# Keys made once per batch in the second cross attention, and the turned means copied by ScalarE

## The chip, the cores and the metric

The kernel runs on one core of a Trainium2 chip. The core has TensorE (matrix products), VectorE, ScalarE (activations) and GpSimd, and SyncE, which here only issues DMAs. Matmuls write PSUM, which has eight banks of 512 float32 per partition; everything else lives in SBUF, 128 partitions. The metric is the device time of one execution in microseconds.

## The reference, cut to what matters

Two layers, each an attention, a cross attention over a context, and a feed-forward part, with layer norms between. The input is 8 batches of 56 tokens of width 128; the context `ctx_512` is 8 batches of 1500 rows of width 64. The change is in the cross attention of the second layer and in what prepares it. With 16 heads of 8 key columns each:

```
qh = (q @ Wq + bq).reshape(B, LQ, HEADS, D_K).transpose(0, 2, 1, 3)
kh = (k @ Wk + bk).reshape(B, LKV, HEADS, D_K).transpose(0, 2, 1, 3)
vh = (v @ Wv + bv).reshape(B, LKV, HEADS, D_K).transpose(0, 2, 1, 3)
scores = jnp.einsum('bhqd,bhkd->bhqk', qh, kh) * (1.0 / np.sqrt(D_K))
attn = jax.nn.softmax(scores, axis=-1)
out = jnp.einsum('bhqk,bhkd->bhqd', attn, vh)
return concat @ Wo + bo
```

## The kernel before, in words

Everything runs in one program, stage after stage; each engine has its own written order, and semaphores tie them. The two cross attentions are two objects of the class `Cross` (L916): `cross1` (first layer) and `cross2` (second layer, `biased`). Both run over 8 batches of 12 chunks; a chunk is 125 context rows against all 16 x 56 = 896 queries.

Keys are never made. The key weights are folded into the queries: the query unit ("Q", L1003) multiplies each head's queries by its key weights, giving 64 rows (and one for the bias), and scores are products of these with the turned context (64 x 1500 per batch). For precision both sides are split in a high and a low bf16 part, stacked on the rows: one matmul of 128 rows and one of 65 (97 in `cross2`), each in two halves of 448 columns (L1125), four per chunk.

In chunk n, TensorE (`run_pe`, L1094) waits for the exp of chunk n-2, issues the scores of n, and then the value sums (`pv`, L1054) of chunk n-2: fourteen matmuls on the high part of the probabilities (L1066, L1068) and seven on the low part (L1073). ScalarE takes the exp (L1206). The low part of the probabilities is made on GpSimd or VectorE (`low_part`, L1226); `low_on_pool` says by whom (in `cross2` before: VectorE in chunks 0, 1 and 11 of a batch). Four buffers (`RING`) hold probabilities.

Between, side units for the next batch are placed by hand (`placement`, L896), each in one of three side banks taken in turn, where a unit waits until the unit three places ahead has been read: queries ("Q"), 21 maxima ("M", a matmul of 500 columns, L1024, and a VectorE reduction, L1241), the shift by the maximum ("A", L1030 and L1253), and for the batch before the turned means ("N", L1036; VectorE copies them, L1270) and the output projection ("O", L1042; copy L1274). The mean itself (`mean`, L1278: L1282 and L1286) is VectorE's, and TensorE starts the value sums of a batch only when it is done.

`cross2` needs the turned context in bf16 parts: SyncE loads it (`turned_in`, L1982), ScalarE copies it (`context_act`, L1182 and L1183), and VectorE or GpSimd makes its low part (`context_low`, L1191). For batches 0 and 1 that is done in the last batch of `cross1`, in chunks 2 to 9. The front of a cross attention (`front_pe`, `front_dve_run`) makes queries and maxima of batch 0 before its first chunk; `keep_warm` (L212) are matmuls whose results nobody reads.

## Time and profile before

| | us |
|---|---|
| median of 3 runs | 669.24 (666.65 to 669.37) |
| the profiled execution's own time | 664.66 |
| its span, first to last instruction | 662.9 |
| first cross attention, last batch | about 300 to 323 |
| second cross attention, front | about 409 to 428 |
| second cross attention, 8 batches | about 428 to 627 |

Times in a row are microseconds from the start of the span. A row of the timeline gives start, duration, engine, line, operation, tiles, and the number of instructions merged in it. The duration of a matmul has a modelled end; distances between starts are the safer reading.

### The profile page before, as it was taken

The numbers are of one execution on the slowest core, as the hardware profiler recorded it, in microseconds if no ns is written. First come the engines' busy times: TensorE is split into PE (matmuls) and PEld (weight loads), VectorE is DVE, ScalarE is ACT, GpSimd is POOL, SyncE is SP. The second block draws the span as 40 slices with busy tenths as digits, with TensorE's granted clock in tenths as the row PEclk, the third lists the DMA queues.
The fourth block names the chain that finished last, engine by engine and source line by source line (L and its number), as shares of the span: only waits on it lengthen the run. The fifth ranks groups of instructions, "written<-read, shape, count | busy, mean of one in ns | idle before, by whom it ended". The sixth has DMA issues, their size and how long they took to land.

```text
span 662.9 us, 19804 instructions
## 1 busy us (share of the span) xinstructions
PE 621.5 (94%) x8743; PEld 464.5 (70%) x8743; DVE 493.9 (75%) x796; ACT 353.0 (53%) x550; POOL 379.3 (57%) x272
## 2 busy tenths in 40 slices
PE   8889898899999999999898979999999999999997
PEld 4566785677777777777776556677777777777774
DVE  3666738799989889896665764877888988977543
ACT  2065663655646646647354316286586586664443
POOL 1362453388888888574220326078988988955400
PEclk9999999999999999999999999999999999999999
DMA  9600003000000002000032000001101100000000
GB/s 267 244 1 3 3 2 134 2 2 3 2 2 2 2 2 95 4 2 2 1 132 120 1 0 1 1 2 48 48 2 49 48 2 2 2 2 2 2 1 15
DMA packets 4657, 20.87 MB, mean 31 GB/s; under 512 B 500, under 2 KB 756, under 8 KB 4572
## 3 DMA queue, kind: packets, MB, share of 16 engines
q1 hardware_dynamic: 4572, 19.60, 8.8%
q8 instruction: 69, 1.13, 0.7%
q14 instruction: 16, 0.13, 0.1%
HBM read 19.37 MB, written 0.23 MB: 30 GB/s over the span
## 4 chain that ended last, share of the span: by engine, by line
PE 72%; DVE 12%; ACT 8%; issue 5%; POOL 2%; DMA 1%; POOLq 0%; DVEq 0%
PE psum L1125 18%; PE psum L1024 10%; PE psum L1066 5%; PE psum L1073 5%; PE psum L212 5%; PE psum L1068 5%; DVE scratch L1241 3%; PE psum L1003 3%; PE psum L1030 1%; PE psum L241 1%; PE psum L1042 1%; POOL scratch L626 1%; ACT scratch L1159 1%; ACT lv L286 1%; PE psum L1036 1%
## 5 line engine op out<-in xcount | busy, mean ns | idle before, releaser
L1226 POOL TENSOR_TENSOR scratch<-scratch 125x896 bf16<-125x896 f32 x136 | 238.5, 1765 | 117.7 <-ACT scratch L1206 117.5
L1206 ACT ACTIVATE scratch<-psum 125x896 f32<-125x896 f32 x192 | 173.1, 915 | 147.0 <-PE psum L1125 145.8
L1241 DVE TENSOR_REDUCE scratch<-psum 128x1 f32<-128x500 f32 x336 | 209.8, 671 | 14.1 <-PE psum L1024 6.4
L1125 PE MATMUL psum<-scratch 128*125 128x448 bf16 (+2 forms) x624 | 143.6, 355 | 0.5 <-ACT scratch L1206 0.2
L1066 PE MATMUL psum<-tok,scratch 125*128 125x65 bf16 x1344 | 108.9, 195 | 1.8 <-DVE kT L1286 1.8
L1068 PE MATMUL psum<-tok,scratch 125*128 125x64 bf16 x1344 | 108.3, 192 | 0.0
L1066 PEld LDWEIGHTS psum<-tok,scratch 125*128 125x128 bf16 x1344 | 95.3, 97 | 15.6 <-issue 2.6
L1024 PE MATMUL psum<-scratch 128*128 128x500 bf16 x273 | 102.3, 375 | 3.3 <-DVE scratch L1241 2.0
L1068 PEld LDWEIGHTS psum<-tok,scratch 125*128 125x128 bf16 x1344 | 90.2, 99 | 16.1
L1125 PEld LDWEIGHTS psum<-scratch 128*125 128x125 bf16 (+2 forms) x624 | 80.0, 136 | 26.1 <-ACT scratch L1206 0.8
L1226 DVE TENSOR_TENSOR scratch<-scratch 125x896 bf16<-125x896 f32 x56 | 68.6, 1227 | 18.1 <-ACT scratch L1206 17.0
L212 PE MATMUL psum<-w_second 128*128 128x256 bf16 x597 | 79.0, 272 | 0.0
L1073 PE MATMUL psum<-tok,scratch 125*128 125x65 bf16 x1344 | 72.5, 194 | 2.8 <-POOL scratch L1226 1.6
L1073 PEld LDWEIGHTS psum<-tok,scratch 125*128 125x128 bf16 x1344 | 61.1, 98 | 16.8 <-POOL scratch L1226 2.4
L212 PEld LDWEIGHTS psum<-w_second 128*128 128x128 bf16 x597 | 56.7, 97 | 19.4 <-issue 7.4
L1024 PEld LDWEIGHTS psum<-scratch 128*128 128x128 bf16 x273 | 26.3, 96 | 11.5 <-DVE scratch L1241 3.8
L1125 PE MATMUL psum<-scratch,nrm 128*125 128x448 bf16 (+1 forms) x144 | 33.2, 356 | 0.0
L1236 DVE TENSOR_TENSOR scratch<-psum,scratch 64x448 bf16<-64x448 f32 x28 | 17.2, 617 | 16.1 <-ACT scratch L1159 16.0
L1353 POOL CAST tok<-raw 125x384 bf16<-125x384 f32 x16 | 13.4, 836 | 27.3 <-DVE xo L1834 12.5
L281 ACT ACTIVATE sq<-psum 128x224 f32<-128x224 f32 (+2 forms) x24 | 8.6, 357 | 36.6 <-PE psum L241 36.4
L1024 PE MATMUL psum<-nrm,scratch 128*128 128x500 bf16 x63 | 23.6, 375 | 1.2 <-DVE scratch L1236 0.6
L1125 PEld LDWEIGHTS psum<-scratch,nrm 128*125 128x125 bf16 (+1 forms) x144 | 18.1, 136 | 5.3
(337 smaller groups left out, 896.7 us busy)
## 6 DMA issues: line engine op xcount, KB each, us to landing
nrm<-turned_dram SPq DMA_DIRECT2D x8, 750.0 KB, 4.6
raw<-ctx_dram SPq DMA_DIRECT2D x4, 672.0 KB
w_third<-fifth_dram SPq DMA_DIRECT2D x3, 636.0 KB, 5.4
w_third<-third_dram SPq DMA_DIRECT2D x2, 844.0 KB, 21.1
w_third<-third_dram SPq DMA_DIRECT2D x2, 843.5 KB, 19.2
w_fourth<-fourth_dram SPq DMA_DIRECT2D x3, 542.5 KB, 5.7
w_first<-first_dram SPq DMA_DIRECT2D x1, 996.0 KB, 4.8
w_second<-second_dram SPq DMA_DIRECT2D x1, 834.0 KB, 6.7
```

The lines of the kernel that those rows point to most:

```text
L212: nc.tensor.matmul(bank(b, 256), constant[:, 0:128], constant, start=True, stop=True)
L1003: mm = nc.tensor.matmul(psum[0:65, self.home(idx + half), 56 * n:56 * n + 56], par(self.wk, 65 * h, 65 * h + 65)[rows, :], qT[rows, j, 56 ...
L1024: mm = nc.tensor.matmul(bank(B, TB), CR["qa", i][:, 128 * r:128 * r + 128], CR["ya", self.context_of(b)][:, TB * t:TB * t + TB], start=Tru ...
L1066: nc.tensor.matmul(psum[:, sums, 65 * r:65 * r + 65], rows, t[:, c, 64:129], start=(c == 0 and r == 0), stop=False, skip_group_check=True)
L1068: nc.tensor.matmul(psum[:, sums, 65 * r:65 * r + 64], rows, t[:, c, 0:64], start=False, stop=False, skip_group_check=True)
L1073: mm = nc.tensor.matmul(psum[:, sums, 65 * r:65 * r + 65], CR["pl"][0:CP, n % RING, 128 * r:128 * r + 128], t[:, c, 64:129], start=False, ...
L1125: mm = nc.tensor.matmul(bank(S + f, HALF, CP), lhs[0:rows, CP * c:CP * c + CP], rhs[0:rows, HALF * f:HALF * f + HALF], start=(rows == 128) ...
L1206: nc.scalar.activation(CR["p"][0:CP, n % RING, :].rearrange("p (f n) -> p f n", f=2), psum[0:CP, S:S + 2, 0:HALF], ACT.Exp).then_inc(self. ...
L1226: ops.tensor_tensor(CR["pl"][0:CP, n % RING, :], CR["p"][0:CP, n % RING, :], p_high(n % RING), ALU.subtract).then_inc(done, 1)
L1236: nc.vector.tensor_tensor(CR["qb", i][0:64, cols], bank(B, HALF, 64), CR["qa", i][0:64, cols], ALU.subtract).then_inc(self.aux_freed, 1)
L1241: nc.vector.tensor_reduce(mxp[:, r, t:t + 1], bank(B, TB), X_AXIS, ALU.max).then_inc(self.aux_freed, 1)
L1353: nc.gpsimd.tensor_copy(tok[i][:, lot, 64:128], src).then_inc(self.tok_high, 1)
```

## The change

In the second cross attention the keys are made: per batch, three matmuls of 500 columns ("K": `x_wk` by the turned context, float32) give 128 rows, 16 heads of 8. ScalarE adds the bias and writes the high bf16 part, VectorE the low part. SyncE then copies them from SBUF to SBUF into four groups of four heads; a group has 96 rows (32 high, 32 low, 32 high again) and a row of ones for the shift. That is twelve copies per third of a batch, 36 per batch. The queries are no longer folded with the key weights: a matmul with a constant ("spread") puts them in the same 96 rows, masked so that a head meets only its own 8 rows. Scores are four matmuls of 97 rows and 224 columns per chunk. Maxima have tiles of 112 queries, eight in place of seven, so 24 units per batch. The keys of batch b+2 are made in batch b (two in chunk 0, one in chunk 9); those of batches 0 and 1 in chunks 6 to 11 of the last batch of the first cross attention, where `context_act` and `context_low` go. TensorE waits there for all six residues before the value sums of the last two chunks. The turned means are copied by ScalarE. GpSimd has the low part of chunk 1 too, and its memsets for the rows of ones go. The fifth pack of weights shrinks. `cross1` keeps its own way of working.

The diff's core:

```diff
-        def low_on_pool(n):
+        def low_on_pool(n, keyed):
+            if keyed:
+                return n % 2 == 0 if n >= CHUNKS * (BATCH - 1) + 3 else n % CHUNKS not in (0, 11)
             return n % 2 == 0 if n >= CHUNKS * (BATCH - 1) + 3 else n % CHUNKS not in (0, 1, 11)
-        def placement(front, outputs, turns):
+        def keyed_placement(front, outputs, keys):
+            at = [[] for _ in range(CHUNKS)]
+            maxima = iter(KEYED[2:2 + MAXIMA * TBLK])
+            def some(c, n):
+                at[c] += [[u] for u in itertools.islice(maxima, n)]
+            if keys:
+                at[0] += [[("K", 0)], [("K", 1)]]
+            if front:
+                at[1] += [KEYED[0:2]]
+                some(2, 3)
+                some(3, 1)
+            if outputs:
+                at[3] += [[]] * (not front) + [[("N", 0)], [("N", 1)]]
+            if front:
+                some(3, 1)
+                for c in range(4, 11):
+                    some(c, 3 if c < 9 else 2)
+                at[11] += [[], [KEYED[-2]], [KEYED[-1]]]
+            if outputs:
+                at[5] += [[("O", 0)]]
+            if keys:
+                at[9] += [[("K", 2)]]
+            return at
...
                 if kind == "Q":
                     if b:
                         self.wait_freed(pe, idx - 2)
-                    else:
+                    elif not self.keyed:
                         pe.wait_ge(self.yb_set, 2)
+                    if self.keyed:
+                        for g in range(GROUPS):
+                            mm = nc.tensor.matmul(psum[0:96, self.home(idx + g // 2), 224 * (g % 2):224 * (g % 2) + 224],
+                                                  par("spread", 96 * g, 96 * g + 96), qT[:, :, 56 * b:56 * b + 56],
+                                                  start=True, stop=True)
+                            if g % 2:
+                                mm.then_inc(self.aux_ready, 1)
+                        return
...
+                elif kind == "K":
+                    mm = self.keys_pe(pe, b, k, B)
+                elif kind == "M" and self.keyed:
+                    t, r = k // MAXIMA, k % MAXIMA
+                    if k == 0 and b:
+                        pe.wait_ge(self.q_high, 2 * b)
+                    elif k == 0:
+                        pe.wait_ge(self.front_act, 1)
+                        pe.wait_ge(self.front_dve, 1)
+                    if r == 0:
+                        pe.wait_ge(keys_loaded[i][t], 192 * (b // 2 + 1))
+                    mm = nc.tensor.matmul(bank(B, TB, QROWS), CR["qa", i][0:64, QROWS * r:QROWS * r + QROWS],
...
+                                          key_group(i, r // 2)[0:64, TB * t:TB * t + TB], start=True, stop=True)
...
+            def keys_pe(self, pe, b, t, B):
+                if b == 0:
+                    pe.wait_ge(loaded["keys"], 16)
+                pe.wait_ge(turned_loaded[t], 16 * (b + 1))
+                return nc.tensor.matmul(bank(B, TB), par("x_wk", rows=64), turned[:, TB * t:TB * t + TB],
+                                        start=True, stop=True)
+            def keys_act(self, act, b, t, B):
+                cols = slice(TB * t, TB * t + TB)
+                if b:
+                    act.wait_ge(keys_loaded[(b - 1) % 2][t], 192 * ((b - 1) // 2 + 1))
+                nc.scalar.activation(key_high[:, cols], bank(B, TB), ACT.Identity, bias=col("x_bk")
+                                     ).then_inc(keys_high, 1)
+            def keys_dve(self, dve, b, t, B):
+                cols = slice(TB * t, TB * t + TB)
+                dve.wait_ge(keys_high, TBLK * b + t + 1)
+                nc.vector.scalar_tensor_tensor(key_low[:, cols], bank(B, TB), col("x_bk"), key_high[:, cols], ALU.add,
+                                               ALU.subtract).then_inc(keys_low, 1)
...
+                        for g in range(GROUPS):
+                            mm = nc.tensor.matmul(psum[0:CP, S + g // 2, 224 * (g % 2):224 * (g % 2) + 224],
+                                                  key_group(i, g)[0:97, CP * c:CP * c + CP],
+                                                  CR["qa", i][0:97, 224 * g:224 * g + 224], start=True, stop=True)
...
+                    if self is cross1 and b == BATCH - 1 and c >= 6:
+                        kb, t = (c - 6) // TBLK, (c - 6) % TBLK
+                        if kb:
+                            pe.wait_ge(keys_low, t + 1)
+                        else:
+                            self.wait_freed(pe, self.index("O", 0, BATCH - 2))
+                        cross2.keys_pe(pe, kb, t, SIDE[t]).then_inc(keys_made, 1)
+                if self is cross1:
+                    pe.wait_ge(keys_low, 2 * TBLK)
...
-                        nc.scalar.activation(CR["qb", i][96:97, cols], psum[64:65, B, 0:HALF], ACT.Copy)
-                    nc.scalar.activation(CR["qa", i][0:64, cols], bank(B, HALF, 64), ACT.Copy)
-                    ins = nc.scalar.activation(CR["qa", i][64:128, cols], bank(B, HALF, 64), ACT.Copy)
+                    ins = nc.scalar.activation(CR["qa", i][0:64, cols], bank(B, HALF, 64), ACT.Copy)
+                    if not self.keyed:
+                        ins = nc.scalar.activation(CR["qa", i][64:128, cols], bank(B, HALF, 64), ACT.Copy)
                     ins.then_inc(self.q_high, 1)
+                elif kind == "K":
+                    act.wait_ge(self.aux_ready, idx + 1)
+                    self.keys_act(act, b, k, B)
+                elif kind == "N" and self.keyed:
+                    act.wait_ge(self.aux_ready, idx + 1)
+                    if k == 0 and b:
+                        act.wait_ge(self.aux_ready, self.index("O", 0, b - 1) + 1)
+                    lo, hi = (0, 512) if k == 0 else (512, 896)
+                    nc.scalar.activation(usb[0:64, lo:hi], bank(B, hi - lo, 64), ACT.Copy).then_inc(self.mean_turned, 1)
...
-                    if self is cross1 and b == BATCH - 1 and c in (2, 4, 6, 8):
-                        cross2.context_act(act, (c - 2) // 4, (c - 2) // 2 % 2)
-                    if self is cross2 and b < BATCH - 2 and c in (4, 6):
-                        self.context_act(act, b + 2, c // 2 - 2)
+                    if self is cross1 and b == BATCH - 1 and c >= 6:
+                        act.wait_ge(keys_made, c - 5)
+                        cross2.keys_act(act, (c - 6) // TBLK, (c - 6) % TBLK, SIDE[(c - 6) % TBLK])
...
-                elif kind == "N":
+                elif kind == "N" and not self.keyed:
...
+                    if self is cross1 and b == BATCH - 1 and c >= 6:
+                        cross2.keys_dve(dve, (c - 6) // TBLK, (c - 6) % TBLK, SIDE[(c - 6) % TBLK])
...
-                    if self is cross2 and b < BATCH - 2 and c in (5, 8):
-                        self.context_low(pool, nc.gpsimd, b + 2, c // 3 - 1)
...
-            def turned_in(b):
-                sp.dma_start(turned[b % TURNED], packs["turned"][:, CTX * b:CTX * b + CTX]
-                             ).then_inc(turned_loaded[b % TURNED], 16)
+            def turned_in(b, t):
+                cols = slice(TB * t, TB * t + TB)
+                sp.dma_start(turned[:, cols], packs["turned"][:, CTX * b + TB * t:CTX * b + TB * t + TB]
+                             ).then_inc(turned_loaded[t], 16)
+            def keys_in(b, t):
+                cols = slice(TB * t, TB * t + TB)
+                for g in range(GROUPS):
+                    rows = slice(32 * g, 32 * g + 32)
+                    for k, part in enumerate((key_high, key_low, key_high)):
+                        sp.dma_start(key_group(b % 2, g)[32 * k:32 * k + 32, cols], part[rows, cols]
+                                     ).then_inc(keys_loaded[b % 2][t], 16)
+            sp.wait_ge(cx_var, 4)
+            sp.dma_start(params["keys"], packs["keys"]).then_inc(loaded["keys"], 16)
+            for t in range(TBLK):
+                turned_in(0, t)
             sp.wait_ge(cross1.tok_set, 2 * BATCH)
-            for b in range(TURNED):
-                turned_in(b)
+            for i in range(2):
+                sp.dma_start(flat[96:97, 2 * CTX * i:2 * CTX * i + 2 * CTX], packs["ones_row"]).then_inc(ones_loaded, 16)
+            for b in range(2):
+                for t in range(TBLK):
+                    sp.wait_ge(keys_low, TBLK * b + t + 1)
+                    turned_in(b + 1, t)
+                    keys_in(b, t)
...
+            for b in range(2, BATCH):
+                for t in range(TBLK):
+                    if t != 1:
+                        for lot in (0, 1) if t == 0 else (2,):
+                            sp.wait_ge(keys_low, TBLK * b + lot + 1)
+                            if b < BATCH - 1:
+                                turned_in(b + 1, lot)
+                    sp.wait_ge(cross2.scores, CHUNKS * (b - 2) + 4 * t + 4)
+                    keys_in(b, t)
```

## Rows read from the trace of the kernel before

**Rows 1.** The page: busy time by engine, and the chain that ended last

```profile
PE 621.5 (94%) x8743; PEld 464.5 (70%) x8743; DVE 493.9 (75%) x796; ACT 353.0 (53%) x550; POOL 379.3 (57%) x272
...
PE 72%; DVE 12%; ACT 8%; issue 5%; POOL 2%; DMA 1%; POOLq 0%; DVEq 0%
```

**Rows 2.** Busy time in two batches: stretch, length, engines, clock, DMA share, GB/s

```profile
482.51:507.96 25.45, 25.11 (x407) 18.79 (x404) 21.70 (x35) 17.08 (x23) 22.92 (x15) 1.00 0.11 33
507.96:533.40 25.44, 25.10 (x407) 18.79 (x405) 21.73 (x35) 17.08 (x23) 22.93 (x15) 1.00 0.11 32
```

**Rows 3.** Timeline of TensorE, chunks with three maxima

```profile
491.64 0.38 PE L1024 MATMUL psum<-scratch 128*128 128x500 bf16 x1
492.28 0.38 PE L1024 MATMUL psum<-scratch 128*128 128x500 bf16 x1
492.50 0.37 PE L1073 MATMUL psum<-tok,scratch 125*128 125x65 bf16 x7
492.71 0.38 PE L1024 MATMUL psum<-scratch 128*128 128x500 bf16 x1
492.92 0.92 PE L1125 MATMUL psum<-scratch 128*125 128x448 bf16 x4
493.68 0.37 PE L1024 MATMUL psum<-scratch 128*128 128x500 bf16 x1
```

**Rows 4.** Timeline of VectorE in one batch, and its low parts by line

```profile
486.73 1.14 DVE L1270 COPY scratch<-psum 64x512 f32<-64x512 f32 x2
487.79 3.58 DVE L1241 TENSOR_REDUCE scratch<-psum 128x1 f32<-128x500 f32 x6
...
492.05 10.09 DVE L1241 TENSOR_REDUCE scratch<-psum 128x1 f32<-128x500 f32 x15 [0.37 <-PE psum L1024]
...
L1226 DVE TENSOR_TENSOR scratch<-scratch 125x896 bf16<-125x896 f32 x56 | 68.6, 1227 | 18.1 <-ACT scratch L1206 17.0
```

**Rows 5.** Timeline of TensorE: float32 matmuls, two instructions each

```profile
334.13 3.29 PE L735 MATMUL psum<-xn,w_third 128*128 128x224 f32 x16 [0.45 <-DVE xn L695]
337.26 3.19 PE L740 MATMUL psum<-kT,w_third 128*128 128x224 f32 x16
...
507.13 1.16 PE L1003 MATMUL psum<-qT,w_third 64*65 64x56 f32 x32
```

**Rows 6.** Timeline of VectorE and ScalarE: nearest operations, and the front

```profile
407.29 0.57 DVE L2150 SCALAR_TENSOR_TENSOR t<-psum,w_fourth,t 128x336 f32<-128x336 f32 x1 [0.16 <-PE psum L758]
411.63 0.62 DVE L1297 TENSOR_TENSOR scratch<-psum,scratch 64x448 bf16<-64x448 f32 x1
...
420.39 1.85 DVE L1241 TENSOR_REDUCE scratch<-psum 128x1 f32<-128x500 f32 x3 [0.38 <-PE psum L1024]
...
508.87 0.54 ACT L1158 ACTIVATE scratch<-psum 64x448 bf16<-64x448 f32 x1
```

**Rows 7.** Timeline of GpSimd: low parts and a context part

```profile
492.11 1.61 POOL L1191 TENSOR_TENSOR nrm<-nrm 64x750 bf16<-64x750 f32 x1
493.69 4.96 POOL L1226 TENSOR_TENSOR scratch<-scratch 125x896 bf16<-125x896 f32 x3
508.24 2.35 POOL L1226 TENSOR_TENSOR scratch<-scratch 125x896 bf16<-125x896 f32 x1 [0.32 <-ACT scratch L1206]
```

**Rows 8.** Timeline of TensorE, last batch of the first cross attention

```profile
310.47 0.95 PE L1125 MATMUL psum<-scratch 128*125 128x448 bf16 x4
311.89 0.95 PE L1125 MATMUL psum<-scratch 128*125 128x448 bf16 x4
322.71 0.39 PE L1073 MATMUL psum<-tok,scratch 125*128 125x65 bf16 x7 [0.97 <-DVE scratch L1226]
```

**Rows 9.** SyncE: issues in the timeline, durations by line, time to landing

```profile
L1983 SPq DMA_DIRECT2D nrm<-turned_dram x8: 327/328/502, 253.8 to 525.7; - x8
...
340.97 1.91 SPq L1970 DMA_DIRECT2D w_third<-fifth_dram  x4
...
out_dram<-t SPq DMA_DIRECT2D x2, 112.0 KB, 1.7
```

321 lines of the change are left out of this document (167 added, 154 removed).

## The prediction

> **What bounds the kernel now.** I read first the busy shares and the chain that ended last: TensorE is busy 94% of the span and carries 72% of the chain [rows 1]. Then the stretches by stage. Each of the middle batches of the second cross attention takes 25.45 us, to the hundredth, and in one of them TensorE is busy 25.11 us, GpSimd 22.92, VectorE 21.70 and ScalarE 17.08 [rows 2]. So that stage is TensorE's, with VectorE and GpSimd close behind. Modelled ends make a matmul's own duration useless here (0.19 us for 65 columns); I use distances between starts. A run of starts in the maxima [rows 3] gives: one maxima matmul of 500 columns 0.21 us, the seven low value matmuls 0.22, the four score matmuls of 448 columns 0.76. The fourteen high value matmuls take 0.43: two maxima matmuls with them between start 0.64 apart [rows 3]. A chunk with three maxima is then 0.76 + 0.43 + 0.22 + 0.63 = 2.04 us, and VectorE's 15 reductions in 10.09 us (0.67 each) follow that pace; its own pace, where matmuls lie ready, is six in 3.58 us, 0.60 each [rows 4]. Keep that number: three reductions are 1.79 us.
>
> **The change in the steady batches.** Matmuls first, TensorE's sum for one batch with keys.
> - Scores: four matmuls of 224 columns in place of four of 448. At 0.19 per 448 columns [rows 3] a half is 0.095, a chunk 0.385 in place of 0.76. Twelve chunks: -4.5 us.
> - Maxima: 24 in place of 21, three times 0.21: +0.6.
> - Queries: the old unit's 32 instructions take 1.16 us, some 1.1 without the modelled end [rows 5]. The new one is four float32 matmuls of 224 columns; sixteen instructions of 224 columns, two per matmul, span 3.13 us (334.13 to 337.26), 0.39 per matmul [rows 5], so 1.56: +0.5.
> - Keys ("K", three per batch, owners 2 to 7): float32, 500 columns, 0.39 x 500 / 224 = 0.87 each: +2.6.
> Sum -0.8 us of 25.45. The maxima for the shift, the turned means and the output stay as they are.
>
> VectorE: 24 reductions in place of 21, +1.8; three key residues. The trace has no such instruction; the nearest are 0.57 us for the same operation on 336 columns and 0.62 for a subtraction from PSUM on 448 [rows 6]; I take 0.70 each (0.6 to 0.8), +2.1. One low part fewer (1.23 in the mean [rows 4]), -1.2, and no turned means (1.14 for both [rows 4]), -1.1. So 21.7 becomes 23.3. ScalarE has two copies of queries in place of six, at 0.54 for 448 columns [rows 6], loses the context copies, and gains three key copies and the two means, about 0.6 each by the same row: 17.1 [rows 2] less 2.2 plus 3.0 less the context copies, so under 18; it costs nothing, but it now stands between TensorE and the next use of a side bank. It copies the means after the exp of chunk 3; the exp behind it, of chunk 4, is not needed for two more chunks, so I cost the move from VectorE at nothing. Without that cover it would cost 1.1 us a batch. GpSimd gains one low part (1.66) and loses two context parts of 1.6 [rows 7]: even.
>
> Now the waits. In the maxima chunks TensorE needs 0.385 + 0.65 + 0.63 = 1.67, VectorE 1.79, GpSimd 1.66 [rows 4, 7]: VectorE falls about 0.12 behind per chunk and is some 1.1 us late when the shift is asked for, of which about 0.5 us shows. At the start of a batch two keys (1.74) and the queries come before any value sum; the mean waits on VectorE behind a low part and two residues, and the old cover (the queries stood between the last value sum and the first of the next batch) is gone: another 0.5 or 0.6. Against about 1.15 us of such holes today (25.45 less 24.3 of matmul demand by the prices above), I get 25.25 per batch, -0.2 (bounds -1.5, if the holes don't grow, to +0.8, if VectorE's lag is paid in full). The six batches 0 to 5 have keys: -1.3 in all. Batch 6 has none: 2.6 us less, -2.8. Batch 7 has neither keys nor maxima: today 1.42 us per chunk by the prices above, now 1.04, twelve chunks, less what the mean and GpSimd's low parts (1.66 each [rows 7]) hold up: -3.7. The front has three more reductions, 1.8 us, less 0.3 for shorter query work, and the four late query matmuls shrink to one, which takes away most of the waits for TensorE that VectorE has there (0.38 us and two shorter ones [rows 6], 0.9 in all): +0.6. **Second cross attention: -7.2 us.**
>
> **The change in the last batch of the first cross attention.** Here keys of batches 0 and 1 are made from chunk 6 on, six units, and the sums of chunks 10 and 11 now wait for the sixth residue. Follow it by the clock. The scores of chunk 6 start at 310.47 and those of chunk 7 at 311.89 [rows 8]. The first key matmul would run 311.9 to 312.8, its copy (0.6) end at 313.5, its residue at 314.3. Only then does SyncE start. Per third of a context it issues one load and twelve copies of 32 rows, and it takes the next third only when all thirteen are out. The copy of key (1, t) waits until the twelve of (0, t) have landed, because they read the same buffer. So 39 issues stand between the first residue and the last copy. What does an issue cost? No transfer of this size from SBUF to SBUF is in the trace. But of all SyncE's issues none is under 0.327 us, whether 78 KB or 996 KB, 8 loads of contexts have a median of 0.328, and back to back four take 1.91, 0.47 each [rows 9]. I take 0.42 (0.37, the least with the step between, to 0.47). 39 x 0.42 = 16.4: the last is out at 330.7 and lands 1.7 us after its issue, as the outputs do [rows 9], at 332.0. Then ScalarE's copy 0.6, VectorE's residue 0.7 and 0.1 of signals: 333.4. The sums of two chunks, 1.3: 334.7. Today the last of them starts at 322.71 and takes 0.22 [rows 8]. **+11.8 us.** It is all on the path: the mean, the projection and the next stage hang on it. Bounds of the issue alone: +9.8 to +13.7. What was there, four pairs of context copies on ScalarE and four subtractions on VectorE, goes; that is inside the sum, which starts from 310.47.
> In the second attention the same 39 issues (16.4 us) fit in a batch of 25 and are asked for a batch later: no cost. If an issue took over 0.64 us they would bind there as well.
>
> The Trainium skill, "DMA: Bandwidth & Descriptors", section "Issuing engines are not separate DMA queues", says that the sequencer's time to initiate a DMA is "usually small relative to the DMA itself". By that rule the 39 issues would fall away beside the landings, and the result would be rival 1's; the SyncE rows above speak against it, at 0.33 us and more.
>
> **Sum.** -7.2 + 11.8 = +4.6. The profiled execution took 664.66 us (span 662.9): 669.3. The median of the three runs is 4.6 above it, at 669.24: **673.8 us**. A difference of 0.5%, 3.3 us, is about what a measurement of this kernel can tell.
>
> **The rivals.**
> 1. *Issues of small copies are cheap* (0.1 us or so). Then the tail is set by TensorE: six chunks of 1.42 + 0.87 = 2.29 from 310.47 end at 324.2, then copy, residue and sums: 326.9, +4.0 and not +11.8. Sum -3.2: 666.0, faster than before. It decides below 0.2 us per issue (39 x 0.2 = 7.8 is about the matmuls' own pace). For: each copy has 32 rows of 1,000 bytes, a quarter of the others' rows. Against: no row under 0.327 whatever the size. 0.22.
> 2. *The batches gain more*: holes don't grow, 24.3 per batch, -0.95 more for each of six. Sum -1.1: 668.1. For: TensorE's demand falls by 0.8, and VectorE has queues of three banks. Against: VectorE's 23.3 plus its waits for ScalarE. 0.12.
> 3. *The batches don't gain*: VectorE, now with 24 reductions, becomes the bound in full, or the low parts on GpSimd, which take 2.35 us and not 1.66 beside VectorE's own [rows 7], hold chunk 1 to 3. +1 per batch for six: 679.8. A variant of the same sign: TensorE stands idle for some 5 us before 333.4 and comes back at its half clock, 1.2 GHz; all rows of before show a granted clock of 1.00 in the cross attentions, so no row prices it; doubling the 1.3 of sums and part of the projection behind it is +1.5 to +3. 0.16.
> 4. Main case, 0.50. Within it the issue's 0.37 to 0.47 and a few tenths per batch give +1 to +8.
>
> **How the numbers follow.** Main case: slower 0.36, same 0.14. Rival 1: faster 0.12, same 0.10. Rival 2: faster 0.06, same 0.06. Rival 3: slower 0.16. Together faster 0.18, same 0.30, slower 0.52. Range: down to 664.5 for rival 1 with batches a little better, up to 680 for rival 3. The main case's own: 670 to 677.
>
> **What would show it.** SyncE: some 290 more issues; their mean, and the distance between twelve of them, decides. In the first attention's last batch: TensorE idle of 4 to 6 us ahead of the last sums, released by the key residue, and ScalarE's key copies waiting for transfers. Batch distance in the second: 25.2, then 22.6, then some 17.8. VectorE's reductions at 0.60 throughout. The turned means on ScalarE with no added wait for them on TensorE. I am wrong if the last sums of the first attention start before 328, or if a batch falls under 24.5 or rises above 26.

## The result, and the profile after

| | before | after |
|---|---|---|
| median | 668.83 us (666.65 to 669.37) | 728.48 us (727.36 to 729.32) |
| ratio, 95% interval | | 1.090 (1.087 to 1.093) |
| span of the profiled execution | 662.9 | 726.6 |

The change makes the kernel 9% slower. The forecast was 673.8, slower by 0.7%; the sign was right and the size wrong by a factor of more than ten. The two medians differ by 59.7 us and the two spans by 63.7; the profiled execution of before was one of its quick ones (664.66 us).

The page of after, busy time by engine and chain by engine and line; it answers to [rows 1]:

```profile
PE 673.5 (93%) x8630; PEld 476.0 (66%) x8630; DVE 510.7 (70%) x815; ACT 335.9 (46%) x528; POOL 360.8 (50%) x263
...
PE 76%; DVE 10%; ACT 5%; issue 3%; SPq 3%; POOL 1%; DMA 1%; DVEq 0%; POOLq 0%; ACTq 0%
PE psum L1069 9%; PE psum L1216 8%; PE psum L1150 6%; PE psum L1157 6%; PE psum L1207 6%; PE psum L216 6%; PE psum L1152 5%; PE psum L1080 4%; SPq L2101 3%; PE psum L1116 3%; DVE scratch L1327 2%; PE psum L1036 2%; PE psum L1099 2%; PE psum L1105 1%; POOL scratch L630 1%
```

TensorE has 113 matmuls fewer in the profile than before (some records can be missing) and is busy 52 us longer. Two lines are new at the head of the chain: the maxima of the second cross attention (L1069, 9%) and SyncE's copies of the keys (SPq L2101, 3%).

Where the time went is read from one instruction per batch, VectorE's reciprocal at the start of the mean, and from two other reciprocals of VectorE that bound the stretch behind the first cross attention (335.93 in before, 361.76 in after) and the start of the second one's front (391.36 and 417.19). The differences between their starts give the account; "first" and "second" are the cross attentions.

| stretch | before | after | difference |
|---|---|---|---|
| up to the last batch of the first | 303.13 | 304.98 | +1.9 |
| last batch of the first | 20.01 | 42.10 | +22.1 |
| the stretch behind it | 12.79 | 14.68 | +1.9 |
| front and batch 0 of the second | 64.83 | 77.17 | +12.3 |
| the next five batches | 127.27 | 153.27 | +26.0 |
| batch 6 | 25.45 | 27.28 | +1.8 |
| batch 7 | 18.16 | 15.89 | -2.3 |

The stretch between the two bounds is 55.43 us in both, and the batches of the first cross attention ahead of its last are alike to 0.1 us. The 1.9 us of the first line are there already at the first of these reciprocals, which starts at 151.62 in after, at 149.75 in before, and between 149.47 and 151.06 in the other kernels below, some of them with the whole change in them. So they look like the scatter of single executions. The busy time of the engines in a steady batch of after (columns as in [rows 2], which it answers):

```profile
525.42:556.47 31.05, 30.66 (x387) 19.96 (x386) 24.18 (x37) 14.70 (x20) 20.30 (x15) 1.00 0.20 52
```

TensorE is busy for 30.66 of 31.05 us, at full clock. So the batches did not grow by waits: the matmuls themselves take longer than the prices that were read from before. The one wait of TensorE above 0.2 us in such a batch is for the mean, in its timeline:

```profile
526.43 0.19 PE L1150 MATMUL psum<-tok,scratch 125*128 125x65 bf16 x1 [0.29 <-DVE kT L1367]
```

The timeline of TensorE in after, in a chunk with three maxima (it answers to [rows 3]):

```profile
540.96 0.60 PE L1207 MATMUL psum<-scratch,nrm 97*125 97x224 bf16 x4
541.49 0.41 PE L1069 MATMUL psum<-nrm,scratch 64*112 64x500 bf16 x1
541.84 0.20 PE L1150 MATMUL psum<-tok,scratch 125*128 125x65 bf16 x1
...
542.25 0.19 PE L1152 MATMUL psum<-tok,scratch 125*128 125x64 bf16 x1
542.37 0.41 PE L1069 MATMUL psum<-nrm,scratch 64*112 64x500 bf16 x1
542.72 0.39 PE L1157 MATMUL psum<-tok,scratch 125*128 125x65 bf16 x7
543.03 0.41 PE L1069 MATMUL psum<-nrm,scratch 64*112 64x500 bf16 x1
543.38 0.41 PE L1207 MATMUL psum<-scratch,nrm 97*125 97x224 bf16 x2
```

From the start of a maxima matmul to the start of the next instruction are 0.35 us, where before had 0.21; and the seven low value matmuls take 0.31 before the next maxima matmul may start, in place of 0.21 to 0.22. The chunk takes 2.42 us (540.96 to 543.38). The forecast had 1.67 for TensorE and 1.79 for VectorE. What is new in the shape is the first number: a maxima matmul now has 64 rows, and its neighbours 97 or 125.

The other loss is in the last batch of the first cross attention. SyncE's issues there, in the timeline of after (start, duration, then how many are merged):

```profile
316.44 0.48 SPq L2092 DMA_DIRECT2D w_first<-turned_dram  x1
316.96 8.25 SPq L2101 DMA_DIRECT2D nrm<-scratch  x12
325.26 0.59 SPq L2092 DMA_DIRECT2D w_first<-turned_dram  x1
325.89 7.56 SPq L2101 DMA_DIRECT2D nrm<-scratch  x12
333.49 0.59 SPq L2092 DMA_DIRECT2D w_first<-turned_dram  x1
334.13 7.56 SPq L2101 DMA_DIRECT2D nrm<-scratch  x12
```

All issues of that line (least, median and most, in ns), the answer to [rows 9]:

```profile
L2101 SPq DMA_DIRECT2D nrm<-scratch x288: 507/591/1847, 317.0 to 650.3; - x144
```

Three of ScalarE's key copies wait for these transfers, 4.63, 6.77 and 6.74 us (the last one here, in the timeline of after), and the first value sum of the last two chunks, in TensorE's, waits for the last residue:

```profile
343.06 0.68 ACT L1123 ACTIVATE scratch<-psum,w_first 128x500 bf16<-128x500 f32 x1 [6.74 <-DMA nrm<-scratch]
```

```profile
344.57 0.24 PE L1150 MATMUL psum<-tok,scratch 125*128 125x65 bf16 x1 [6.13 <-DVE scratch L1129]
```

The busy time and the clock in four stretches of 10 us of after (the third number from the right is the granted clock):

```profile
310.00:320.00 10.00, 10.00 (x151) 6.37 (x147) 5.07 (x6) 5.73 (x7) 3.91 (x3) 1.00 0.08 21
320.00:330.00 10.00, 6.10 (x55) 3.29 (x54) 2.56 (x3) 3.08 (x4) 2.81 (x2) 0.84 0.23 61
330.00:340.00 10.00, 4.96 (x28) 2.59 (x27) 1.83 (x2) 1.49 (x2) 0.00 (x0) 0.50 0.23 60
340.00:350.00 10.00, 5.43 (x51) 5.15 (x52) 1.57 (x3) 0.68 (x1) 0.00 (x0) 0.50 0.22 56
```

TensorE stands idle for 8.9 of the 20 us from 320 to 340, and its granted clock goes to 0.50, the 1.2 GHz level, and is still there when the sums and the projection run after 344.57.

### The profile page after: what moved, and what is told of

It reads as the page before. It is cut to its first block, busy times and chain, and to the rows that moved or that the text cites. A ratio compares the mean times of both kernels' runs of the same rounds, so it can differ in the third digit from the quotient of the medians.

```text
span 726.6 us, 19924 instructions
## 1 busy us (share of the span) xinstructions
PE 673.5 (93%) x8630; PEld 476.0 (66%) x8630; DVE 510.7 (70%) x815; ACT 335.9 (46%) x528; POOL 360.8 (50%) x263
## 4 chain that ended last, share of the span: by engine, by line
PE 76%; DVE 10%; ACT 5%; issue 3%; SPq 3%; POOL 1%; DMA 1%; DVEq 0%; POOLq 0%; ACTq 0%
PE psum L1069 9%; PE psum L1216 8%; PE psum L1150 6%; PE psum L1157 6%; PE psum L1207 6%; PE psum L216 6%; PE psum L1152 5%; PE psum L1080 4%; SPq L2101 3%; PE psum L1116 3%; DVE scratch L1327 2%; PE psum L1036 2%; PE psum L1099 2%; PE psum L1105 1%; POOL scratch L630 1%
## 5 line engine op out<-in xcount | busy, mean ns | idle before, releaser
L1327 DVE TENSOR_REDUCE scratch<-psum 112x1 f32<-112x500 f32 (+1 forms) x360 | 232.2, 674 | 35.2 <-PE psum L1069 26.2
L1216 PE MATMUL psum<-scratch 65*125 65x448 bf16 (+1 forms) x384 | 89.3, 358 | 0.1
L1069 PE MATMUL psum<-nrm,scratch 64*112 64x500 bf16 x192 | 79.7, 415 | 0.3 <-issue 0.3
L1157 PEld LDWEIGHTS psum<-tok,scratch 125*128 125x128 bf16 x1344 | 57.6, 98 | 25.4 <-issue 16.4
L1310 DVE TENSOR_TENSOR scratch<-scratch 125x896 bf16<-125x896 f32 x48 | 59.8, 1247 | 12.9 <-ACT scratch L1291 12.3
L1080 PE MATMUL psum<-scratch 128*128 128x500 bf16 x168 | 62.9, 375 | 2.1 <-DVE scratch L1327 2.0
L1216 PEld LDWEIGHTS psum<-scratch 65*125 65x125 bf16 (+1 forms) x384 | 49.3, 137 | 19.8 <-ACT scratch L1291 3.0
L1207 PE MATMUL psum<-scratch,nrm 97*125 97x224 bf16 x384 | 55.0, 268 | 0.3 <-DVE scratch L1335 0.3
L1207 PEld LDWEIGHTS psum<-scratch,nrm 97*125 97x125 bf16 x384 | 37.0, 136 | 15.9 <-issue 14.5
L1129 DVE SCALAR_TENSOR_TENSOR scratch<-psum,w_first,scratch 128x500 bf16<-128x500 f32 x24 | 17.7, 738 | 35.9 <-ACT scratch L1123 35.6
L1069 PEld LDWEIGHTS psum<-nrm,scratch 64*112 64x112 bf16 x192 | 23.6, 123 | 21.2 <-issue 6.5
L1116 PE MATMUL psum<-w_first 64*128 64x500 f32 x48 | 28.0, 668 | 7.4 <-DVE scratch L1129 3.9
```

The lines of the kernel that those rows point to most:

```text
L1069: mm = nc.tensor.matmul(bank(B, TB, QROWS), CR["qa", i][0:64, QROWS * r:QROWS * r + QROWS], key_group(i, r // 2)[0:64, TB * t:TB * t + TB] ...
L1080: mm = nc.tensor.matmul(bank(B, TB), CR["qa", i][:, 128 * r:128 * r + 128], CR["ya", i][:, TB * t:TB * t + TB], start=True, stop=True)
L1116: return nc.tensor.matmul(bank(B, TB), par("x_wk", rows=64), turned[:, TB * t:TB * t + TB], start=True, stop=True)
L1157: mm = nc.tensor.matmul(psum[:, sums, 65 * r:65 * r + 65], CR["pl"][0:CP, n % RING, 128 * r:128 * r + 128], t[:, c, 64:129], start=False, ...
L1207: mm = nc.tensor.matmul(psum[0:CP, S + g // 2, 224 * (g % 2):224 * (g % 2) + 224], key_group(i, g)[0:97, CP * c:CP * c + CP], CR["qa", i][ ...
L1216: mm = nc.tensor.matmul(bank(S + f, HALF, CP), lhs[0:rows, CP * c:CP * c + CP], rhs[0:rows, HALF * f:HALF * f + HALF], start=(rows == 128) ...
```

## The experiments

The theory made from the two traces: the loss is (a) about 0.23 us for each maxima matmul, because its 64 rows stand between matmuls of over 64, and (b) an issue of a copy from SBUF to SBUF takes 0.63 us on SyncE and not 0.42, in a chain of 39 that halts TensorE. Rivals: maxima or scores are slowed by where they read or write (the keys now lie in the token buffer, filled by transfers), by VectorE, or by the copies' traffic; and the turned means on ScalarE hold the side banks. Each kernel is compared with executions of the kernel before on the same chip (medians 667.2 to 667.7).

One thing has to be known for all of them. Many of these kernels show short stretches at the 1.2 GHz level, most of them 3 to 4 us long, and they don't come in the same places: before with its maxima over 64 rows has one at 332 to 336, and the kernel behind it, with the same code there, has none at that place but one at 396 to 400. Most of them cost 1 to 1.6 us. So distances are compared where the granted clock is 1.00, and where it isn't the text says so.

### Maxima over 96 rows

After, with the maxima over 96 rows of the same keys and queries; the rows 64 to 95 add the low part of the products, so the maxima must wait for the queries' low parts.

```diff
-  CR["qa", i][0:64, QROWS * r:QROWS * r + QROWS], key_group(i, r // 2)[0:64, TB * t:TB * t + TB]
+  CR["qa", i][0:96, QROWS * r:QROWS * r + QROWS], key_group(i, r // 2)[0:96, TB * t:TB * t + TB]
```

> The changed kernel, with the maxima matmuls over 96 rows of queries and keys in place of 64 (the low rows of the queries join; TensorE waits for them ahead of the first maximum). Theory A, a matmul over 64 rows between matmuls over more rows costs TensorE about 0.23 us more than its columns do: each of the 24 maxima per batch goes from 0.44 to 0.21 us, 5.5 us less per batch, so the distance of two batches falls from 31.05 to about 25.5, and the whole to about 690 us. Rival B, the 36 copies per batch from SBUF to SBUF, or their reading, slow TensorE or the reductions: the copies are the same here, so the distance stays at 31 and the whole at 728. The halt ahead of the last sums of the first attention (to 347) stays under both.

Measured: 703.6 us, ratio 1.054 (1.047 to 1.060); span 701.0, 25.6 less than after. TensorE's timeline in this kernel, one chunk with three maxima:

```profile
523.94 0.55 PE L1207 MATMUL psum<-scratch,nrm 97*125 97x224 bf16 x4
524.32 0.38 PE L1069 MATMUL psum<-nrm,scratch 96*112 96x500 bf16 x1
524.97 0.40 PE L1069 MATMUL psum<-nrm,scratch 96*112 96x500 bf16 x1
525.42 0.40 PE L1069 MATMUL psum<-nrm,scratch 96*112 96x500 bf16 x1
525.65 0.55 PE L1207 MATMUL psum<-scratch,nrm 97*125 97x224 bf16 x4
```

1.71 us in place of 2.42, and the prediction's 1.67 for TensorE is confirmed: the same matmul of 500 columns with half as many rows again is cheaper by 0.71 / 3 = 0.24 us. Batches take 27.71, 3.35 less. They don't take 25.3: TensorE is busy 25.22, and the maxima now wait for the queries' low parts, once a batch, in this kernel's timeline (0.55 more is a wait for the shift; with 64 rows after has neither):

```profile
542.27 0.39 PE L1069 MATMUL psum<-nrm,scratch 96*112 96x500 bf16 x1 [1.94 <-DVE scratch L1377]
```

### Maxima over 64 rows in the kernel before

The same thing from the other side: nothing of the change, only the maxima of the second cross attention over the rows 64 to 127 (the low part of the context is left out of them).

```diff
-  CR["qa", i][:, 128 * r:128 * r + 128], CR["ya", self.context_of(b)][:, TB * t:TB * t + TB]
+  rows = slice(64, 128) if self.biased else slice(0, 128)
...
+  CR["qa", i][rows, 128 * r:128 * r + 128], CR["ya", self.context_of(b)][rows, TB * t:TB * t + TB]
```

> The kernel before, with one size changed: the maxima of the second cross attention are taken over 64 rows (the high parts alone, so the shift is a little off the true maximum) in place of 128. No key copies exist here. Theory A: 21 x 0.23 = 4.8 us more per batch, distance 25.45 to about 30.3 for the seven batches with maxima, the whole from 669 to about 703. Rival B: half the rows cost nothing, distance 25.45 or below, 669.

Measured: 699.7 us in one execution, span 697.9, 35 us over before. Batches take 29.70 in place of 25.45: 4.25 / 21 = 0.20 us per maxima matmul. The front and batch 0 take 72.78 in place of 64.83, so the front loses 3.7 as well. Its stretch behind the first attention is 1.05 longer too (13.84, granted 0.88), which is one of the low stretches and not the maxima. No key, no copy between buffers and no other place of operands is in this kernel, so (a) needs none of them.

### The matmuls around them over 64 rows too

Is it the change between shapes, or is a 64-row matmul slow? In the front of the kernel before, three unread matmuls of `keep_warm` stand between two maxima. Here they have 64 rows like the maxima.

```diff
-  nc.tensor.matmul(bank(b, 256), constant[:, 0:128], constant, start=True, stop=True)
+  nc.tensor.matmul(bank(b, 256), constant[rows, 0:128], constant[rows], start=True, stop=True)
...
-  keep_warm(3 if k else 8, 2 if self.biased else 6)
+  keep_warm(3 if k else 8, 2 if self.biased else 6, rows=slice(64, 128) if self.biased else slice(0, 128))
```

> The kernel before with the second cross attention's maxima over 64 rows (as e2_before_max64), and the three unread matmuls that stand between two maxima in the front over 64 rows too. Starts of the front's maxima are 0.54 us apart with 128 rows everywhere and 0.75 where only the maxima have 64 rows. Theory 'a change of the number of row groups costs, about 0.1 us each way': with both at 64 rows the distance returns to 0.54 (at most 0.60), while the batches behind, where the maxima still stand between wider matmuls, stay at 29.7 us. Rival 'a maxima matmul over 64 rows is slow in itself, or its operands in this place are': the distance stays at 0.75 or grows to 0.8 and more, since the others are narrow now as well. The whole is some 3.5 us under e2_before_max64's 699.7: 696 by the first, 700 or more by the second.

TensorE's timeline in the front, of the kernel with 64 rows in the maxima alone, and of the one with 64 rows in all:

```profile
414.24 0.38 PE L1025 MATMUL psum<-scratch 64*128 64x500 bf16 x1
414.56 0.50 PE L212 MATMUL psum<-w_second 128*128 128x256 bf16 x3
414.99 0.38 PE L1025 MATMUL psum<-scratch 64*128 64x500 bf16 x1
```

```profile
414.20 0.37 PE L1025 MATMUL psum<-scratch 64*128 64x500 bf16 x1
414.41 0.48 PE L212 MATMUL psum<-w_second 64*128 64x256 bf16 x3
414.74 0.37 PE L1025 MATMUL psum<-scratch 64*128 64x500 bf16 x1
```

0.75 us from one maximum to the next becomes 0.54, exactly the distance in before with 128 rows everywhere. The maxima matmul is the same in both, 64 rows from the same place; only its neighbours differ. So the price is for the change between 64 rows and more (96 to 128 in these kernels), some 0.1 us each way, and not for the 64 rows. The batches stay at 29.7, as expected.

The whole took 699.4 (one execution, span 697.6), 0.3 under the other kernel and not 3.5, and front and batch 0 together fell only from 72.78 to 71.58. The maxima don't miss the gain. From the first of the front's 21 maxima matmuls to the last are 14.23 us here (413.66 to 427.89), 17.59 in the other kernel (413.49 to 431.08) and 13.05 in before (411.81 to 424.86): 3.36 us were won, as expected. The 1.2 over before fit the four late query matmuls of 128 rows between them, where the rows still change: two maxima with one of those between stand 1.40 apart here and 1.10 to 1.12 in before. What was won was lost outside the maxima, in two stretches at the 1.2 GHz level that this execution has and the other doesn't. Their clock in this kernel (the third number from the right):

```profile
396.00:398.00 2.00, 2.00 (x11) 1.22 (x10) 1.47 (x4) 0.61 (x2) 0.28 (x1) 0.56 0.00 0
432.00:434.00 2.00, 2.00 (x8) 1.17 (x6) 0.00 (x0) 0.80 (x1) 0.00 (x0) 0.55 0.00 0
```

The first lies ahead of the maxima, in code that is the same in both, and counted from the start of the front they begin 0.95 us later; the second lies between the last maximum and the first value sum, which are 8.27 us apart in place of 7.06. That is 2.2 of the 3.4 us. So the time of one execution would have spoken against the theory, and the distances between starts decide for it.

The Trainium skill, "TensorEngine Tiling (Array Packing)", section "Key Properties", has a line that fits: "Changing tiling mode (not just tile) drains the TensorE". The traces show a cost of 0.1 us and a little more at each change between 64 rows and more, as such a drain would give. That a plain matmul over 64 rows is such a change of mode no run here shows. The prediction did not use this line.

### Key matmuls over 128 rows

After, with the key matmul over 128 rows, of which the 64 added ones meet weights of zero.

```diff
-  par("x_wk", rows=64), turned[:, TB * t:TB * t + TB]
+  par("x_wk"), params["first"][:, TB * t:TB * t + TB]
```

> The changed kernel, the 24 key matmuls over 128 rows (64 of them meet weights of zero) in place of 64. Theory A: each of them is followed and preceded by matmuls over more rows; by 0.2 us each, 0.6 per batch with keys, distance 31.05 to 30.45, and 5 us less in the whole at most, about 723. If the surcharge for the narrow form is bound to short bf16 matmuls only, nothing: 728.

Measured: 724.5 us in one execution, span 722.7. Batches take 30.63, 0.42 less for three keys: 0.14 each. From start to start a key matmul takes 0.92 us (512.33 to 513.25) in place of 1.03 (545.47 to 546.50). The same cost as with the maxima: 0.09 to 0.11 behind each key and 0.08 to 0.09 ahead of two of them; the first key of a batch, behind a matmul of the shift, starts 0.29 behind it in both kernels and shows none ahead.

### A buffer of its own for the second batch of keys

After, but the keys of batch 1 have parts of their own, so that their copies on ScalarE wait for no transfer, and all three context loads go ahead of the 36 copies of batch 0.

```diff
-                if b:
-                    act.wait_ge(keys_loaded[(b - 1) % 2][t], 192 * ((b - 1) // 2 + 1))
+                if b == 2:
+                    act.wait_ge(keys_loaded[0][t], 192)
+                elif b > 2:
+                    act.wait_ge(keys_loaded[(b - 1) % 2][t], 192 * ((b - 1) // 2 + 1))
```

> The changed kernel, but the keys of batch 1 get a buffer of their own and SyncE issues the three context loads of batch 1 ahead of the copies of batch 0, so nothing in the last batch of the first attention waits for SyncE's 39 issues. Theory C, the issues (0.63 us each) are the whole of the halt: the mean after the last sums starts at about 329 in place of 347, the half clock between 327 and 350 goes, 18 to 20 us less, about 709. Rival D, the key units themselves or ScalarE's order hold that batch: less than 5 us gained. The batch distance in the second attention stays 31 under both.

Measured: 712.4 us, ratio 1.067 (1.060 to 1.073), span 711.3. The last batch of the first attention takes 26.87 in place of 42.10, the stretch behind it 13.40 in place of 14.68; busy time and clock in the first of them in this kernel, and below it SyncE's issues in its timeline:

```profile
303.70:330.57 26.87, 24.41 (x341) 16.99 (x341) 13.56 (x17) 13.23 (x16) 9.00 (x5) 0.96 0.12 33
```

```profile
320.83 24.46 SPq L2108 DMA_DIRECT2D nrm<-scratch  x36
```

The 36 issues still take 24.46 us, but nobody waits for them. So 15.2 of the 22.1 us were the wait for the copies and what it did to the clock, 16.5 with the stretch behind. The 6.9 that are left are longer matmuls, since TensorE is busy 24.41 in place of 17.21: six keys (6 x 1.03 = 6.2), and about one more by a stretch at the 1.2 GHz level that remains (granted 0.55 from 328 to 330). The next kernels, with keys over 128 rows and a clock of 1.00 there, have 24.5.

### What an issue costs

The kernel before with more transfers on SyncE at a time when it has nothing to do (their data are not used): twelve loads from HBM and twelve copies from SBUF to SBUF, all of 32 rows of 1,000 bytes, three copies of 128 rows, and four of 32 rows of 3,000 bytes.

```diff
+            for k in range(3):
+                for rows in four:
+                    sp.dma_start(block[k][rows], packs["turned"][rows, 250 * k:250 * k + 250]).then_inc(probed, 16)
...
+                    sp.dma_start(block[3 + k][rows], block[k][rows]).then_inc(probed, 16)
...
+                sp.dma_start(block[k], block[3 + k]).then_inc(probed, 16)
...
+                sp.dma_start(flat[rows, 3 * CTX + 750:3 * CTX + 1500], flat[rows, 3 * CTX:3 * CTX + 750]).then_inc(probed, 16)
```

> The kernel before, with extra DMAs on SyncE at about 255 us where it has 86 us to wait: 12 loads from HBM of 32 rows x 1,000 bytes, then 12 copies from SBUF to SBUF of the same form, 3 copies of 128 rows x 1,000 bytes, 4 copies of 32 rows x 3,000 bytes, each group after the one before has landed. What sets SyncE's issue time? If the form from SBUF to SBUF does: 0.33 to 0.47 for the loads, 0.63 for all copies. If the number of rows or bytes does: copies of 128 rows differ from those of 32. If only the length of the queue does: the first issues of each group near 0.35, the later ones longer, whatever the form. The time of the whole stays at 669.

Issues of the four kinds in this kernel (least, median and most, in ns):

```profile
L1994 SPq DMA_DIRECT2D nrm<-turned_dram x12: 421/424/1449, 255.2 to 261.7; - x12
L1998 SPq DMA_DIRECT2D nrm<-nrm x12: 559/591/1729, 263.6 to 271.7; - x12
L2001 SPq DMA_DIRECT2D nrm<-nrm x3: 518/601/603, 273.5 to 274.7; - x3
L2004 SPq DMA_DIRECT2D nrm<-nrm x4: 556/592/593, 278.5 to 280.3; - x4
```

A load costs 0.42, a copy between places in SBUF 0.59, whether it has 32 rows or 128, 1,000 bytes a row or 3,000. For copies the size doesn't matter; the longest issue in each of the two groups of twelve takes 1.4 and 1.7 us. The price of the prediction, 0.42, is right for this load, which is the form that its rows had. The form is not all, though: SyncE's loads of a third of the context take 0.59 (median) between copies in after, and 0.47, the same instruction, in the kernel by way of HBM that has no such copies; the whole contexts in before took 0.33 [rows 9]. The kernel took 667.0, so the probe itself costs nothing.

### The turned means on VectorE

After, with that part of the change undone.

```diff
-                elif kind == "N" and not self.keyed:
+                elif kind == "N":
+                    if self.keyed:
+                        ins = nc.vector.tensor_copy(usb[0:64, lo:hi], bank(B, hi - lo, 64))
```

> The changed kernel with one part undone: VectorE copies the turned means of the second attention, as before, and ScalarE does not. Theory E, the move is hidden: TensorE sets the batch (its switches), VectorE has 5 us of holes in 31, so distance 31.05 and the time stay within 2 us of 728. Rival F, VectorE is short in chunks 3 to 5: 1.1 us per batch more, 8 us in the whole, 736. Rival G, the copies on ScalarE hold its exps back: 1 us per batch less, 720.

Measured: 727.5 us, ratio 1.089 (1.085 to 1.094): no difference from after (728.5). The batches are 31.05 and 31.04, as with ScalarE. In after ScalarE does both in 1.03 us between two exps, in its timeline:

```profile
529.96 1.03 ACT L1268 ACTIVATE scratch<-psum 64x512 f32<-64x512 f32 x2 [0.41 <-PE psum L1099]
```

The exp behind them (at 531.38) still waits 0.39 us for its scores, so the means cost it nothing. With TensorE's surplus gone (next section) the same part was tried again.

### All of it together, in another order

After with the maxima over 96 rows, the keys over 128 and the own buffer; and, against the 1.94 us of wait that the first brought, VectorE's low parts of the queries ahead of the mean and the first maximum of a batch behind the high value sums. Its twin has the turned means on VectorE.

```diff
+                    if self.keyed and c == LAG - 1:
+                        for unit in units:
+                            self.dve_unit(dve, *unit)
+                        units = []
...
+                at[2] += [[]]
```

> The changed kernel with four repairs together: maxima over 96 rows, key matmuls over 128 rows, a buffer of its own for the keys of batch 1 with its loads ahead, and, against TensorE's wait of 1.9 us for the low part of the queries that the first repair brought in, VectorE takes these lows ahead of the mean and TensorE the first maximum behind the high value sums. By the parts measured so far: 728 - 25 (maxima, with its new wait) - 16 (buffer) - 3 (keys) = 684; the order brings 1.5 to 2.2 us for each of seven batches, 10 to 15, and ends the half clock: about 671. Batch distance 25.5 to 26. If the key copies had a price of their own in the second attention, the distance stays above 27 and the whole above 680.

> The kernel of e9_order with VectorE copying the turned means in place of ScalarE: the same question as in e6_means_vector, where TensorE no longer pays for switches and VectorE is close to its limit (about 23 of 25.5 us per batch). Theory E: the copies fall beside TensorE's work all the same, within 2 us of e9_order. Rival F: VectorE's 1.1 us per batch shows, 5 to 8 us more than e9_order.

Measured: 678.3 us, ratio 1.016 (1.011 to 1.020), and the twin 679.7, ratio 1.018 (1.012 to 1.023). The two intervals overlap: the means on ScalarE may be worth 1.4 us here, and the runs don't show it. Batches alternate between 27.07 and 28.38. The busy time and the clock in one of each, in this kernel:

```profile
465.05:492.12 27.07, 24.69 (x385) 19.47 (x385) 22.92 (x37) 14.83 (x20) 20.32 (x15) 1.00 0.23 59
492.12:520.50 28.38, 26.23 (x385) 20.60 (x385) 23.02 (x38) 14.42 (x20) 20.33 (x15) 0.94 0.23 58
```

Both long batches hold a stretch at the 1.2 GHz level; TensorE's matmuls take 1.5 us longer in them, more than the whole difference of 1.3. SyncE's timeline in this kernel runs almost without a gap (0.83 us is the longest between 454 and 604):

```profile
497.00 17.20 SPq L2111 DMA_DIRECT2D nrm<-scratch  x24
514.25 0.59 SPq L2101 DMA_DIRECT2D w_first<-turned_dram  x1
514.89 8.51 SPq L2111 DMA_DIRECT2D nrm<-scratch  x12
523.44 1.23 SPq L2101 DMA_DIRECT2D w_first<-turned_dram  x2
524.72 16.15 SPq L2111 DMA_DIRECT2D nrm<-scratch  x24
```

These 39 issues take 27.7 us (497.00 to 524.67), which is the mean of the two distances, so with the maxima repaired they bind at least in part: a key copy on ScalarE waits 1.06 us for a transfer of the batch ahead (at 543.68). The mean behind such a copy comes later, and the value sum's wait for it is 1.69 and 1.76 us where the clock then falls, 1.45 in the other batches. The twin has a batch of 28.28 at a clock of 1.00 throughout.

### The keys by way of HBM

As the kernel just told, but per third SyncE stores the two parts (two issues) and loads them back with three, each for four groups at once: 6 issues with the context load, not 13.

```diff
-                for g in range(GROUPS):
-                    rows = slice(32 * g, 32 * g + 32)
-                    for k, part in enumerate((high, low, high)):
-                        sp.dma_start(key_group(b % 2, g)[32 * k:32 * k + 32, cols], part[rows, cols]
-                                     ).then_inc(keys_loaded[b % 2][t], 16)
+                for k in range(3):
+                    dst = flat[32 * k:32 * k + 32, at:at + 2 * CTX].bitcast(BF16).rearrange("p (g c) -> p g c", g=GROUPS)
+                    src = keys_mem[b, k % 2].rearrange("(g p) c -> p g c", g=GROUPS)
+                    sp.dma_start(dst[:, :, cols], src[:, :, cols]).then_inc(keys_loaded[b % 2][t], 16)
```

> The version of e9_order, but the keys go to their 96 rows by way of HBM: per third of a batch SyncE stores the two parts (128 rows x 500 bf16 each) and loads them back with three transfers (32 rows, four groups at once), so 6 issues with the context load in place of 13. In e9_order SyncE's queue runs without a gap through the middle batches (6 + 2 + 24 + 1 + 12 issues from 491.92 to 523.4). Theory 'the issues bind there': SyncE is busy some 18 x 0.42 = 7.6 us of a batch, ScalarE's key copy waits for no transfer, the alternation 27.1 / 28.4 goes, and batches settle at 26.0 to 26.5; five of them and the front give -8 us: 670 (666 to 673). In the first attention's last batch each third pays two landings (1.9 each) instead of 7.6 of issues, so the distance stays near 24.5. Rival 'the batches are bound at their start by TensorE's order (keys, queries, mean)': the distances stay at 27.1 and the time near 677; the half-clock stretches stay too. Rival 'HBM trips are late': a wait for nrm appears on TensorE at the first maximum, and the time is over 680.

Measured: 676.1 us, ratio 1.011 (1.008 to 1.014). The alternation is gone and batches take 26.80 to 26.82 at a clock of 1.00: 0.9 less than the mean of 27.7 and not the 1.5 expected, of which 0.27 is the gain against a batch at full clock; the rest came with the low stretches, which these batches don't have, and the runs don't show what the issues had to do with them. Batch 0 with the front grew by 1.3 (69.85 in place of 68.51), but not by the trips to HBM: VectorE's work in the two fronts is the same to 0.02 us for 37 us, and then this execution has a low stretch (granted 0.60 and 0.55 from 434 to 438) and is 1.34 behind. The engines in one batch of this kernel, and, in its timeline, the wait of a batch's first value sum for the mean:

```profile
493.85:520.65 26.80, 24.66 (x385) 19.43 (x385) 22.91 (x37) 14.65 (x20) 20.31 (x15) 1.00 0.30 85
```

```profile
494.86 0.19 PE L1159 MATMUL psum<-tok,scratch 125*128 125x65 bf16 x1 [1.44 <-DVE kT L1376]
```

TensorE is busy 24.66, 0.45 less than in before [rows 2], and stands idle for 2.14 us where before has 0.34. What the keys gain on TensorE is given back to two waits, 1.44 for the mean and 0.70 for the shift. Most of the first is of this version's own making: its order puts VectorE's two low parts of the queries (492.66 to 493.85, 1.19 us) ahead of the mean, and in after, where the mean goes first, the same wait is 0.29.

### One key later, and the queries behind the last sums

Two ways against that wait. The first moves a key matmul from the start of a batch to chunk 10:

```diff
-                at[0] += [[("K", 0)], [("K", 1)]]
+                at[0] += [[("K", 0)]]
...
-                at[9] += [[("K", 2)]]
+                at[9] += [[("K", 1)]]
+                at[10] += [[("K", 2)]]
```

> The version of e11_through_hbm with one key in chunk 0, one in chunk 9 and one in chunk 10, in place of two in chunk 0 and one in chunk 9. Theory 'the start of a batch is where TensorE waits for the mean': a key less in chunk 0 (0.92 us of TensorE ahead of the mean's last sums, 0.74 of VectorE ahead of the mean) moves to chunk 10, where only two maxima stand: -0.3 to -0.9 us per batch for five batches, 1.5 to 4 us in all below e11_through_hbm. Rival 'TensorE's sum binds everywhere': no difference (within 1 us). Rival 'the key in chunk 10 is late for the next batch's maxima': TensorE waits for nrm there, slower by up to 1 us a batch.

Measured: 677.6 us, ratio 1.016 (1.012 to 1.020), no gain: a miss. The wait for the mean grew from 1.44 to 1.64: what was moved away lay ahead of it and did not make it shorter. In three of the four middle batches (28.03, 28.05 and 28.05) the granted clock fell behind that wait to 0.50 (mean 0.94); the one without has 26.47, behind a wait of 1.66 us like the others, which is 0.3 better than 26.80. So at full clock the move brought the least that was expected, and the low stretches took it. Stretches of 2 us of this kernel around it:

```profile
492.00:494.00 2.00, 1.52 (x24) 1.18 (x25) 1.00 (x3) 0.00 (x0) 1.55 (x1) 0.86 0.34 77
494.00:496.00 2.00, 2.00 (x19) 1.61 (x18) 1.68 (x4) 0.89 (x1) 0.00 (x0) 0.50 0.84 233
```

The second puts work over the wait: the four query matmuls (1.6 us) come behind the last value sums of the batch ahead, so that TensorE has them to do while VectorE makes the mean. VectorE's mean goes ahead of the low parts again, as in after, and the maxima of chunk 2 go behind both value sums.

```diff
-                at[1] += [KEYED[0:2]]
-                at[2] += [[]]
+                at[1] += [[], [], KEYED[0:2]]
+                at[2] += [[], []]
```

> The version of e11_through_hbm with the queries' matmuls of a batch behind the last value sums of the batch ahead (chunk 1) in place of ahead of them, VectorE's mean ahead of the query lows, and the maxima of chunk 2 behind both value sums. In e11_through_hbm TensorE stands 1.44 us a batch for the mean (matmuls 24.66 of 26.80 us), and the four query matmuls (1.6 us) lie ahead of the sums that the mean waits for. Theory 'the lost cover of the mean is what is left of the batches': the wait goes under 0.4 us, batches come to 25.4 to 25.9, four of them and the next give -4 to -6 us, 671 (669 to 673), about 0.5% above the kernel before. Rival 'the first maxima now wait for the query lows': the wait moves to the maxima of chunk 2, batches stay at 26.5 or more, 675 or more.

Measured: 672.3 us, ratio 1.005 (1.003 to 1.008). Batches take 26.27; in its middle batches the wait for the mean is gone, and 0.50 us of waiting for the queries' low parts is new:

```profile
521.84 0.81 PE L1076 MATMUL psum<-nrm,scratch 96*112 96x500 bf16 x3 [0.50 <-DVE scratch L1386]
```

So the wait went, and the rival held too, for half a microsecond: 26.27 lies between the 25.4 to 25.9 of the one and the 26.5 of the other. Two things changed at once, the cover on TensorE and the order on VectorE; with the low parts' 1.19 us no longer ahead of the mean, most of the 1.44 would go without any cover, and no run parts the two. This is the best version with keys that was found. It is 56 us faster than after and still 0.5% slower than before. Its last batch of the first attention takes 24.51 (before 20.01), the front with batch 0 69.36 (64.83, with low stretches in it: granted 0.95), batches 1 to 4 0.8 each more, batch 5 0.7 less, batches 6 and 7 2.3 less each.

## Why the prediction was wrong

The direction rested on the first attention's last batch, and that mechanism was right. The step that failed was in the other part: for the second cross attention the prediction forecast a gain of 7.2 us, and it lost 37.9. That the sign of the whole came out right is the first attention's work alone.

**Steady batches: predicted 25.25, measured 31.05.** The failed step is "Maxima: 24 in place of 21, three times 0.21": 0.21 was the distance in before, for 128 rows between 97 to 128 rows [rows 3], and was carried over to 64 rows between the same neighbours. The 64 rows stood in the diff (`[0:64, ...]`), and no row of before showed a maxima matmul of that shape; the prediction drew no bound for it. Per three maxima TensorE needs 2.42 and not 1.67, times eight: +6.0. With three keys at 1.03 in place of 0.87, +0.5, that is more than the whole miss of 5.8; the VectorE lag of 1.1 us, expected as the next bound, disappears behind the slower TensorE (its reductions wait for matmuls, in after, by about 0.2 us each time). With 96 rows the chunk took 1.71, as costed.

**The holes: predicted +0.5 to +0.6 each.** In after TensorE is idle 0.39 us a batch, 0.29 of it for the mean: the slower maxima cover both. With 96 rows the wait for the shift is 0.55, as told, and 0.68 to 0.70 in the reordered versions. The wait for the mean of 1.44 in those has VectorE's low parts ahead of it, which the change itself has not; the 1.94 with 96 rows is for low parts that 64 rows don't need. So what the change would be worth without the switch and without a new wait was not run. But for one batch of 28.28, all versions have batches of 26.3 to 27.7 at full clock, near rival 3's +1 a batch, but not by its cause: VectorE is busy 22.8 to 23.1 of them and GpSimd 20.3, and it is single waits at the start and the end of a batch that fill the rest.

**Front: predicted +0.6, measured +6.7** (77.17 less a batch of 31.05, against 64.83 less 25.45). With 96 rows it is 1.7: 5.0 were the change of rows.

**Batch 6: predicted 22.65, measured 27.28.** It has no keys but 24 maxima; the versions with 96 rows and another order have 22.25 to 23.1, about as costed. **Batch 7**, without maxima: predicted a gain of 3.7, measured 2.3. The value sums at 1.42 less 0.38 a chunk were right for TensorE, busy 13.7 of 15.9; the rest waits.

**First attention's last batch: predicted +11.8, measured +22.1 and 1.9 behind it.** By its own chain, shifted by the 1.9 us by which after starts later: the first issue was expected at 316.2 and is at 316.44. 39 issues were to take 16.4 and take 25.25 (316.44 to 334.13 + 7.56), 0.65 each: +8.9. Then copy, residue and sums follow as told (344.57 where 335.3 was expected), and end 1.0 later still at half clock. The failed term is the issue of 0.42; "no transfer of this size from SBUF to SBUF is in the trace" was said, and the bound of 0.47 was then drawn from loads alone. The half clock was named as a variant with 1.5 to 3; it came to 1.0 and at most 1.9, of which not all need be the halt's, since a kernel without any halt lost 1.05 in the same stretch (13.84). Rival 1 falls: the sentence of the Trainium skill ("DMA: Bandwidth & Descriptors", "Issuing engines are not separate DMA queues") that stood beside it is not borne out here, at 0.59 for the issue of a copy that lands in 1.9. "If an issue took over 0.64 us they would bind there as well" was borne out in kind: at 0.65 to 0.71 from one to the next SyncE had almost no gap left once the batches were short.

**Small parts.** Two sums of the prediction don't hold, without bearing on the miss. If the holes don't grow, a batch is 25.45 - 0.8 = 24.65, not rival 2's 24.3 and not 1.5 less, and rival 2 is 670.2 rather than 668.1. GpSimd, told as even, loses 1.5 a batch by the prediction's own prices (two times 1.6 less 1.66) and went from 22.9 to 20.3. VectorE's key residue 0.74 (0.70 told), ScalarE's key copy 0.68 (0.6 told), VectorE's busy time without the switch 23.0 a batch (23.3 told). The turned means on ScalarE cost nothing, as forecast, and bring nothing either.

The account closes: first attention with what is behind it +12.2 over the forecast, batches 0 to 5 +32.9, front +6.1, batch 6 +4.6, batch 7 +1.4, and +1.9 ahead of all that, from the first 150 us: 59.1, the 63.7 measured less the 4.6 forecast.

**What stays open.** Why the front with the first batch remains 3.7 to 5 us longer in the versions with keys was not followed (it has three more reductions, 1.8 us, batch 0's own 0.8 to 2.3, and in two of three a low stretch). Why the clock falls in one execution and not in another of the same code, at the same waits, stays open too. No version removed the six key matmuls from the first attention, where ScalarE's and VectorE's old work was hidden and theirs is not.

## What to carry to other kernels

Before a matmul is given fewer rows, look at its neighbours' rows: going to 64 rows and back cost 0.24 us here, and the 500 columns themselves 0.21. So fill up the rows where the matmuls around are wide, with zeros, or with parts that are ready in time. Price an issue by a row of the same form, and where there is none, measure it first: dozens of small copies on one queue are a chain. When work is taken from a stage, ask which latency it had covered. And before two executions are compared, look at the granted clock of each stretch: low stretches hid most of a gain of 3.4 us here and feigned a loss of 1.3.

## What the runs showed of the hardware

- A matmul of 500 columns over 64 rows between matmuls of more rows takes 0.20 (against 128 rows) to 0.24 us (against 96) more of TensorE; between matmuls of 64 rows it takes nothing more (0.54 from one maximum to the next, not 0.75). Both ways share it: about 0.14 behind it and 0.1 ahead. In the profile it shows as busy time, not as a wait.
- A float32 matmul of 500 columns takes 0.92 us at 128 rows between wide ones, 1.03 at 64.
- SyncE issues a copy from SBUF to SBUF in 0.59 us, 32 rows or 128, 1,000 bytes a row or 3,000; a load from HBM in 0.33 (whole contexts), 0.42 or 0.47, and in 0.59 between such copies; a store to HBM in 0.44 (medians). The copies follow each other at 0.63, with a long one now and then, 0.65 to 0.71 in the mean.
- The clock fell to the 1.2 GHz level behind waits of TensorE of 1.64 us (492.48, the kernel with one key later; granted 0.50 at 494 to 496) and of 1.94 us (542.27, maxima over 96 rows; 0.50 at 544 to 546), which made those batches 1.6 us longer. The same waits stand in other batches of the same two executions (1.66 at 520.53, 1.94 at 514.57) with the clock at 1.00, and behind 1.44 us (the kernel by way of HBM) it stayed there in all six.
